# Attention in a transformer block: queries and keys turned as plain rows and spread over partitions by transfers, with the projections cut into pieces

## What is computed

```
q, k, v = split(layernorm(x) @ Wqkv + bqkv)        # 16 heads of 16
q, k = rot(q), rot(k)                              # t1*c - t2*s, t1*s + t2*c
scores = einsum('bthd,bshd->bhts', q, k / 4)
attn = softmax(scores + causal_mask)
x = x + (einsum('bhts,bshd->bthd', attn, v) @ Wout + bout)
```

## Time and profile before

| | |
|---|---|
| runs | 1165.92, 1167.31, 1172.52 us; median 1167.31 |
| profiled execution | 1165.93 us, its span 1164.0 |
| TensorE busy | 1052.2 us, 90% |
| VectorE, ScalarE, GpSimd busy | 731.1, 463.2, 432.6 us |
| TensorE's granted clock, mean | 0.935 of full |
| attention stage | from 198.3 us to about 531 us of the span |

### The profile page before, as it was taken

One profiled execution on the slowest core, in us unless ns is written; L12 is line 12 of the kernel. 1 busy time (PEld: TensorE's weight loads), 2 busy tenths in 40 slices (PEclk: granted clock), 3 DMA queues, 4 the chain that ended last, 5 costly groups with the idle time before them and its releaser, 6 DMA issues. The chain is left out here.

```text
span 1164.0 us, 18769 instructions
## 1 busy us (share of the span) xinstructions
PE 1052.2 (90%) x6537; PEld 870.1 (75%) x6537; DVE 731.1 (63%) x1754; ACT 463.2 (40%) x806; POOL 432.6 (37%) x474
## 2 busy tenths in 40 slices
PE   4899995779999999987999987999988998899997
PEld 3778884656566665666888886888878897788886
DVE  7934443787777778557454446765648878555653
ACT  4324331327666756625243322233334434223222
POOL 3056654326362723201576521000139788300000
PEclk8699998889989998887999998999997999999999
DMA  9034422300000000117472241000010030000000
GB/s 335 31 94 144 156 80 90 108 0 2 2 1 20 1 19 19 37 37 290 143 252 91 83 162 61 1 1 1 1 73 1 4 70 1 1 1 19 19 19 19
DMA packets 36881, 72.39 MB, mean 62 GB/s; under 512 B 8180, under 2 KB 25654, under 8 KB 36536
## 3 DMA queue, kind: packets, MB, share of 16 engines
q1 hardware_dynamic: 29112, 50.21, 12.8%
q0 software_dynamic: 7680, 20.98, 5.5%
HBM read 47.04 MB, written 24.13 MB: 61 GB/s over the span
## 5 line engine op out<-in xcount | busy, mean ns | idle before, releaser
L2041 PE MATMUL ps<-xt,w 128*128 128x512 f32 x768 | 192.5, 401 | 7.0 <-PEq L66 7.0
L2041 PEld LDWEIGHTS ps<-xt,w 128*128 128x128 f32 x768 | 143.3, 192 | 36.9 <-issue 5.5
L1740 DVE CUSTOM_DVE_ANT_0 ps<-ps,att_mask 128x128 f32<-128x128 f32 (+3 forms) x256 | 119.1, 516 | 40.6 <-PE ps L1343 40.3
L718 PE MATMUL ps<-moe_w,moe_narrow_xb 128*128 x480 | 125.0, 395 | 0.0
L122 POOL TENSOR_TENSOR var_eps<-bn,eps 128x4 f32<-128x4 f32 x24 | 6.6, 275 | 290.5 <-DVE bn L99 265.5
L2137 DVE TENSOR_TENSOR had_gated<-ps,had_sig 128x512 f32<-128x512 f32 x64 | 44.3, 691 | 110.8 <-ACT had_sig L2094 110.8
L2094 ACT ACTIVATE had_sig<-ps 128x512 f32<-128x512 f32 x64 | 38.3, 598 | 188.7 <-PE ps L2041 188.7
L616 POOL DMA_INDIRECT moe_xs<-xn_rows,moe_index x80 | 80.7, 1009 | 75.5 <-DVE moe_index L1017 44.1
L622 POOL DMA_INDIRECT made_rows<-moe_units_made,moe_index x80 | 79.6, 994 | 74.6 <-ACT moe_units_made L845 62.1
L718 PEld LDWEIGHTS ps<-moe_w,moe_narrow_xb 128*128 128x128 f32 x480 | 90.1, 188 | 19.6
L1606 ACT ACTIVATE att_early_probs<-ps 128x384 f32<-128x384 f32 (+1 forms) x192 | 90.7, 527 | 29.4 <-PE ps L1358 28.5
(11 more groups left out here) (276 smaller groups left out, 2320.0 us busy)
## 6 DMA issues: line engine op xcount, KB each, us to landing
moe_w<-in_moe SPq DMA_DIRECT2D x16, 768.0 KB, 8.9
back<-made_rows SPq DMA_DIRECT2D x16, 512.0 KB, 5.7
x<-x_turned SPq DMA_DIRECT2D x8, 512.0 KB, 7.9
low_weights<-moe_w SPq DMA_DIRECT2D x4, 768.0 KB, 3.6
moe_w<-low_weights SPq DMA_DIRECT2D x4, 768.0 KB, 16.7
x<-in_x SPq DMA_DIRECT2D x4, 512.0 KB, 5.5
xn_rows<-moe_wide_xn SPq DMA_DIRECT2D x4, 512.0 KB, 10.7
x_turned<-x SPq DMA_DIRECT2D x4, 512.0 KB, 2.9
```

The lines of the kernel that those rows point to most:

```text
L718: last = nc.tensor.matmul(h_bank(j, i), xb[a][:, j % 2, i, k, :], weight(c), start=False, stop=(k == KC - 1 and c == 1))
L1740: last = nc.vector.tensor_tensor_reduce(g.ps[:, a, col:col + n], g.ps[:, a, col:col + n], mask[:, SEQ - n:SEQ], -1.0, 3.0e38, ALU.add, ALU ...
L2041: last = nc.tensor.matmul(g.ps[:, bank(n, half), :], w[a][:, k, c * P:(c + 1) * P], xt[low][:, b % 2, k, :], start=(k == 0 and q == 0), st ...
```

## The change

The stacked operands in token rows (`q_stack`, `k_stack`) go, and with them `high`, `low`, `out_q1`, `out_q2`, `out_k` and the three turns of each pair. In their place:

1. The rotated rows are turned as they are, in *chunks*: chunk n = 4 b + c is 128 columns (8 heads) of the queries (c even) or keys (c odd) of batch b, four blocks in one bank (`turn_chunk`). ScalarE writes the high part into `stage`, VectorE the low part. Two stores put both into DRAM (`spread_dram`), and six loads (two heads' halves a, three places c) each bring rows into 16 partitions of `qt` or `kt`, all pairs of the chunk at once. `kt` is filled with ones once, for the fourth place.
2. The shift no longer goes through the stack: `maxima` writes into `shift`, `turn_shift` turns it with four products of two columns, ScalarE evicts two rows, and two transfers of one row each put them into `qt`. The shifted scores wait for them (`shift_here`).
3. The first pair of the first batch is copied straight from `stage` (`direct_here`), queries from SP's queue and keys from ScalarE's; GpSimd does all half-swaps; `rope_a` scales `qk` in place.
4. The projections are cut into pieces over more steps, `weigh` is split 3 to 1 instead of 2 to 2, two value tiles share a bank and an eviction, and the norm of the batch after next moves from u = 19 and 22 to 5 and 7 on VectorE.

Other banks and waits follow from these. The core of the diff:

```diff
-        rot = turns("rot", [P, 2, 2 * D])
...
-        part_b = sb("part_b", [P, 2, 2 * D])
+        rot = sb("rot", [P, BT, 2 * D])
+        stage = sb("stage", [P, 2, 2, SEQ], F32R)
+        shift = sb("shift", [P, 3, BT, 2], F32R)
+        shift_row = sb("shift_row", [P, SEQ], F32R)
+        ident_r = sb("ident_r", [P, P], F32R)
         v = sb("v", [P, 2, BT, H, HD + 1])
-        q_stack = sb("q_stack", [P, 2, BT, H, SK], F32R)
-        k_stack = sb("k_stack", [P, 2, BT, H, SK], F32R)
-        q1 = sb("q1", [P, 2, SEQ], F32R)
-        q2 = sb("q2", [P, 2, SEQ], F32R)
-        kt = sb("kt", [P, 4, SEQ], F32R)
+        qt = sb("qt", [P, 2, H // 2, SEQ], F32R)
+        kt = sb("kt", [P, 2, H // 2, SEQ], F32R)
...
+        COPIES = ((0, 1, 0), (0, 0, 1))
+        CHUNK_BANK = 4
+        LEAD_CHUNKS = 2
+        stacked = (qt, kt)
+
+        CHUNK_TURNS = {2: 2, 5: 3}
+        for b in range(1, BATCH):
+            begin = WIDTH * (b - 1)
+            CHUNK_TURNS.update({begin + 17: 4 * b, begin + 18: 4 * b + 1, begin + 23: 4 * b + 2, begin + 26: 4 * b + 3})
+
+        def chunks_turned(t):
+            return LEAD_CHUNKS + sum(turned < t for turned in CHUNK_TURNS)
+
+        def shift_turned_at(t):
+            return (t - 4) // STEPS if t >= 4 and (t - 4) % STEPS == 0 and (t - 4) // STEPS < BATCH * PAIR else None
+
...
+        def copies(n):
+            for a in range(2):
+                for c, half in enumerate(COPIES[n % 2]):
+                    yield a, slice(64 * a + HD * c, 64 * a + HD * (c + 1)), half
...
+            def store_chunk(n):
+                b, c = n // 4, n % 4
+                sp.wait_ge(chunk_hi, n + 1)
+                sp.wait_ge(chunk_lo, n + 1)
+                if b:
+                    sp.wait_ge(rows_here[c], 96 * b)
+                for half in range(2):
+                    sp.dma_start(g.spread_dram[c, half], f32(stage[:, n % 2, half, :])).then_inc(stage_stored[n % 2], 16)
+
+            def load_chunk(n):
+                b, c = n // 4, n % 4
+                begin = 1 if n < LEAD_CHUNKS else 0
+                sp.wait_ge(stage_stored[n % 2], 32 * (n // 2 + 1))
+                sp.wait_ge(ones_set, min(b, 1) + 1)
+                if b >= 2:
+                    sp.wait_ge(st_ps, 2 * STEPS * PAIR * (b - 1))
+                for a, rows, half in copies(n):
+                    mine = g.spread_dram[c, half].rearrange("(m a d) n -> a d m n", a=2, d=HD)[a]
+                    sp.dma_start(f32(stacked[n % 2][rows, b % 2, 4 * (c // 2) + begin:4 * (c // 2) + 4, :]),
+                                 mine[:, begin:, :]).then_inc(rows_here[c], 16)
+
+            def place_shift(w):
+                b, hp = w // PAIR, w % PAIR
+                sp.wait_ge(shift_out, w + 1)
+                for a in range(2):
+                    at = 64 * a + 3 * HD
+                    sp.dma_start(f32(qt[at:at + 1, b % 2, hp, :]), f32(shift_row[a:a + 1, :])).then_inc(shift_here, 16)
...
+            sp.wait_ge(chunk_hi, 1)
+            sp.wait_ge(chunk_lo, 1)
+            for a, rows, half in copies(0):
+                sp.dma_start(f32(qt[rows, 0, 0, :]), f32(stage[HD * a:HD * (a + 1), 0, half, :])).then_inc(direct_here[0], 16)
+            for n in range(LEAD_CHUNKS):
+                store_chunk(n)
+            for n in range(LEAD_CHUNKS):
+                load_chunk(n)
+            BESIDE = {2 * WIDTH + 2: (store_x, 0), 3 * WIDTH + 2: (store_x, 1), 3 * WIDTH + 11: (store_xn, 0),
+                      3 * WIDTH + 20: (store_xn, 1)}
+            for t in range(ALL + LAG):
+                if shift_turned_at(t - 1) is not None:
+                    place_shift(shift_turned_at(t - 1))
+                if t - 2 in CHUNK_TURNS:
+                    load_chunk(CHUNK_TURNS[t - 2])
+                if t - 1 in CHUNK_TURNS:
+                    store_chunk(CHUNK_TURNS[t - 1])
+                if t in BESIDE:
+                    store, b = BESIDE[t]
+                    store(b)
...
+            def turn_rows(n, i):
+                kind, half = n % 2, n % 4 // 2
+                at = kind * D + half * P
+                return nc.tensor.transpose(g.ps[:, chunk_bank(n), i * P:(i + 1) * P], rot[:, i, at:at + P], g.ident[:, :])
+
+            def turn_chunk(n, t):
+                pe.wait_ge(rot_done, BT * (n // 4 + 1))
+                if shifts_turned(t):
+                    pe.wait_ge(shift_out, shifts_turned(t))
+                pe.wait_ge(chunk_hi, n)
+                pe.wait_ge(chunk_lo, n)
                 for i in range(BT):
-                    flat = f32(stack[:, b % 2, i, :, :]).rearrange("p h c -> p (h c)")
-                    last = nc.tensor.transpose(g.ps[:, bank, i * P:(i + 1) * P], flat[:, hp * P:(hp + 1) * P],
-                                               g.ident[:, :])
-                last.then_inc(done, 1)
-
-            def turn_q1(w):
-                pe.wait_ge(lo_done, 4 * (w // PAIR) + 4)
-                if w >= 3:
-                    pe.wait_ge(q2_out, w - 2)
-                turn_stack(w, q_stack, 4, q1_ps)
-
-            def turn_k(w):
-                pe.wait_ge(q1_out, w + 1)
-                turn_stack(w, k_stack, 4, k_ps)
-
-            def turn_q2(w):
+                    last = turn_rows(n, i)
+                last.then_inc(chunk_ps, 1)
+
+            def turn_shift(w, t):
+                pe.wait_ge(cleared, 2)
                 pe.wait_ge(max_done, 2 * STEPS * (w + 1))
-                pe.wait_ge(k_out, min(w + 3, BATCH * PAIR))
-                turn_stack(w, q_stack, 4, q2_ps)
+                pe.wait_ge(chunk_hi, chunks_turned(t))
+                pe.wait_ge(chunk_lo, chunks_turned(t))
+                if w:
+                    pe.wait_ge(shift_out, w)
+                for i in range(BT):
+                    last = nc.tensor.matmul(g.ps[0:2, CHUNK_BANK, i * P:(i + 1) * P], shift[:, w % 3, i, :],
+                                            ident_r[:, :], start=True, stop=True)
+                last.then_inc(shift_ps, 1)
...
+                elif step == 0:
+                    for kind in range(2):
+                        pe.wait_ge(rows_here[2 * (hp // 4) + kind], 96 * (b + 1))
...
-                    pe.wait_ge(q2_out, w + 1)
+                    pe.wait_ge(shift_here, 32 * (w + 1))
...
-                if step == 0 and s + 1 < BATCH * PAIR:
-                    turn_q1(s + 1)
-                elif step == 1 and s + 1 < BATCH * PAIR:
-                    turn_k(s + 1)
-                elif step == 2 and 1 <= s <= BATCH * PAIR:
-                    turn_q2(s - 1)
...
-                        project_qk(front, 0, 6)
+                        project_qk(front, 0, 6, range(0, 1))
                     elif u == 4:
-                        project_qk(front, 1, 5)
+                        project_qk(front, 0, 6, range(1, 4))
+                    elif u == 5:
+                        project_qk(front, 0, 6, range(4, 7))
+                        project_qk(front, 1, 5, range(0, 3))
+                    elif u == 6:
+                        project_qk(front, 1, 5, range(3, 7))
                     elif u == 7:
                         pe.wait_ge(qk_out, 4 * front + 1)
-                        project_qk(front, 2, 6)
-                    elif u == 8:
+                        project_qk(front, 2, 6, range(0, 3))
+                    elif u == 9:
+                        project_qk(front, 2, 6, range(3, 5))
+                    elif u == 10:
+                        project_qk(front, 2, 6, range(5, 7))
                         pe.wait_ge(qk_out, 4 * front + 2)
-                        project_qk(front, 3, 5)
+                        project_qk(front, 3, 5, range(0, 1))
+                    elif u == 11:
+                        project_qk(front, 3, 5, range(1, 7))
...
+                if shift_turned_at(t) is not None:
+                    turn_shift(shift_turned_at(t), t)
+                if t in CHUNK_TURNS:
+                    turn_chunk(CHUNK_TURNS[t], t)
...
+            def high_chunk(n):
+                act.wait_ge(chunk_ps, n + 1)
+                if n >= 2:
+                    act.wait_ge(stage_stored[n % 2], 32 * (n // 2))
+                if LEAD_CHUNKS <= n < 2 * LEAD_CHUNKS:
+                    act.wait_ge(direct_here[n % 2], 96)
+                nc.scalar.activation(stage[:, n % 2, 0, :], g.ps[:, chunk_bank(n), :], ACT.Copy).then_inc(chunk_hi, 1)
+
+            def out_shift(w):
+                act.wait_ge(shift_ps, w + 1)
+                if w:
+                    act.wait_ge(shift_here, 32 * w)
+                nc.scalar.activation(shift_row[0:2, :], g.ps[0:2, CHUNK_BANK, :], ACT.Copy).then_inc(shift_out, 1)
...
-            def out_k(w):
-                dve.wait_ge(k_ps, w + 1)
-                if w >= 4:
-                    dve.wait_ge(st_ps, 2 * STEPS * (w - 3))
-                nc.vector.tensor_copy(kt[:, w % 4, :], g.ps[:, 4, :]).then_inc(k_out, 1)
+            def low_chunk(n):
+                dve.wait_ge(chunk_hi, n + 1)
```

(4 more changed lines are left out.)

343 lines of the change are left out of this document (146 added, 197 removed).

## The result

The changed kernel takes 1197.45 us (median of 4 runs, 1192.80 to 1201.82) against 1169.91 us for the kernel before, run beside it: a ratio of 1.0231, 95% interval 1.0168 to 1.0294. It is slower, by 27.5 us. The forecast was 1193. Its profiled execution took 1196.2 us, 30.3 more than the one of before.

A forecast was written before the change was run, and what follows sets the result against it. TensorE, busy for 90% of the span, was taken to bound the kernel, with late transfers next. The sum 1165.9 - 30 - 4 + 49 + 11 = 1191.9 gave 1193 us against the median; range for 8 in 10: 1146 to 1222.

The forecast's parts named there:

- its own range: Whole kernel: the range of the main forecast, 1178 to 1206 us, for 1.0 to 1.4 us a transfer; chance 0.50.
- The loop's work: Attention loop: the longer of TensorE's and VectorE's work, summed over 96 steps, falls from 230.9 to 200.7, 30 us less.
- the step that took TensorE's other pieces at one price before and after: Attention loop: scores, weighings and projections were priced per piece, such as 0.61, 1.63 and 1.80 us, in both kernels' sums.
- the shift's four products: Attention loop: 8 turns of the shift a batch, four products each, put at 0.3 us, 2.4 us a batch.
- the even shares: Attention loop: projections cut into pieces even the steps; step 3 of a batch falls from 4.54 to 1.83 us.
- the missing turns: Attention loop: the change takes out 24 turns of 0.5 us a batch, 12.0 us of TensorE's work.
- The transfers, 49 + 11 us: SP's queue: late loads and shifts make TensorE wait 16.4 us a batch, three times (49), and 11 in the opening.
- The transfer into 16 partitions: Loads on SP's queue: 128 KB into 16 partitions take 1.2 us, 7.2 a load; ends 0.4 and 2.8 a transfer.
- A store landing late behind a load: SP's queue: a sign that the forecast is right; store B lands at 15.3 us and load B is waited for 4.4.
- The opening, 4 us earlier: Ahead of the loop: first scores at 231 to 232 instead of 236.65, taken as 4 us less, ends 0 and 5.
- The rival with the clock: Loop: waits idle TensorE, its clock falls from 0.92 to 0.8, adding 26 us, 1219 in all; chance 0.14.

## Why the prediction was right, and where not

The time, 1197, lies 4 us above the forecast of 1193, on its side and in its own range. Point by point the agreement is worse than that.

**The loop's work, 30 us less: failed.** Measured without transfers to wait for, the third batch is 1.4 us shorter than before and the last 3.3 longer. The turns that went are worth what the sums said, 7.5 us of TensorE's time in the third batch against 7.6. What failed is the step that took TensorE's other pieces at one price before and after. With less to do TensorE was granted less clock (0.74 in the last batch against 0.88, with no transfer waited for; idle products brought 0.94), and its scores, shifted scores and weighings took 43.5 us there in the place of 33.1. In the third batch, at the same mean clock, they took 3.2 us more; why, is not shown. Two smaller things were left out. The chain that the change makes (TensorE turns a chunk, ScalarE evicts it, VectorE subtracts ahead of its maxima) gives VectorE 16.6 us of waiting, of which TensorE's longer waits for maxima, under 6 us in two batches, are what can reach the time. And the shift's four products, taken as 0.3 us, take 0.36 to 0.56 from their start to the next one. Of the two halves of the term, the even shares are real (9.2 us of loop by themselves, on the kernel before); the missing turns gave nothing that the time of any run shows: the third batch takes 63.4 us with the whole change and 61.9 with the even shares alone.

**The transfers, 49 + 11 us: the mechanism held, the size was too large.** The waits stand where the text put them, near the ends of batches and at step 3 of the first, the longest 5.2 us. In the opening they are 6.0 us in the place of 11 (4.0 at step 3 in the place of 6.4, 2.0 for a shift row in the place of 4.4), behind it 25.9 in the place of 49; 2.3 more, for the direct transfers, belong to the start of the first scores. The transfer into 16 partitions took 1.0 us, not 1.2; that TensorE's slower steps also gave each load more time is likely, but not measured. As a price for the whole time two batches' loads cost some 18 us in one pair of kernels and some 6 in another, and waits that went by another order brought no time. The Trainium skill (SBUF — State Buffer, the DMA port swizzle) gives 104 GB/s for partitions 0 to 15, measured with a transfer of 1 MiB; the rows here have 131 to 146 GB/s for a train of six such transfers of 128 KB into six groups of partitions. No run has one alone, so the skill's figure is neither confirmed nor refuted; for a train the measured rate decides, and the 1.2 us taken here was too long. The alternating order left the rate at 131.

**"A store landing late behind a load"** is right, and shown by SyncE's queue: the second load could be issued only at 297.56. But the order was not the cause of the lateness, as the kernel with the stores first shows.

**The opening, 4 us earlier: 2.1 us.** The first scores came at 234.53, after 2.3 us of waiting for the direct transfers.

**The rival with the clock** came true in its condition: 0.81 in the loop, where it said 0.8. Its reason, that the waits leave TensorE idle, is not the whole one: the last batch has 0.74 without waits for transfers. Its price was not worked out rightly either (12% of 230 is 27.6, and going from 0.92 to 0.8 lengthens work by 15%, 35 us), and it stood on top of a forecast whose 30 us of gain the same clock took back. In the measured loop the clock and the waits share 23 us, and the runs do not set them apart; the idle products brought the clock back to 0.91 and the loop, with 278.3 us, grew by 10.

**Behind the loop** the prediction had nothing, and the profiles differ by 9.2 us, which is no more than the same stretch varies on one chip. The largest piece is the features stage, between the issue of its two large transfers: 76.5 us before (853.2 to 929.7), 83.8 after (877.8 to 961.6). The mean of its granted clock is 0.91 in the one and 0.83 in the other (nine windows of 10 us each); it stands at 0.50 from 883 to 893 us before and from 887 to 907 after, with TensorE busy throughout.

In short: the sum had +26 us, 60 of waits less 30 of work and 4 for the opening. The profiles show +30: 23.0 in the loop, 1.7 less ahead of it, 9.2 behind it. Put in the same form, the loop's 23.0 are 31.9 of waits less 8.9 of all the rest, the clock included: two terms that missed by 28 and 21 us to opposite sides. That the time came within 4 us of the forecast is luck; what was right is the direction, and the transfers as a cause.

## What to carry to other kernels

Before a layout is made by transfers in the place of an engine, multiply its bytes by the rate for the partitions that one transfer reaches, and hold that against the time between the layout's source and its use: here 1.57 MB had 7.7 us at 137 GB/s, and neither another queue nor another order helped. Where two engines hand work to and fro in steps, cut the largest pieces first: with the same work it gave 0.5% here. A sum of the longer of two engines' work is a lower bound: price it also at the clock that the engine gets when it has less to do, and put a new operation that a third engine must finish first into it as a chain. And do not add up waits as prices: here 14 us of them went, and the loop stayed as long.

## What the runs showed of the hardware

A train of transfers of 128 KB, each from DRAM into 16 partitions in rows of 2 KB, keeps all 16 DMA engines occupied (share 1.08 to 1.12) and still moves only 131 to 146 GB/s, in both orders of partitions that were tried. The same 24 weighing products took 2.60 us at the lower level of TensorE's clock and 1.49 at the upper. A whole last batch of the same work took TensorE 52.2 us at a mean clock of 0.75 and 40.5 at 0.92, and the 112 records of idle products that kept the clock up took 14.7, so the batch was no shorter (60.9 and 61.9 us). In the kernel before with even shares, the last batch, with the same code, took 53.2 us at 0.94 on one chip and 56.9 at 0.85 on another.
